# The low halves of V: from VectorE reading PSUM to GpSimd reading a 32-bit copy that ScalarE writes

## The chip, the cores and the metric

The kernel runs on one core of a Trainium2 chip. Its metric is the device time in microseconds (us) of one execution of the whole program, here one launch that holds two attention layers and two feed-forward layers. The engines of the core are called PE (TensorE, matmuls; PEld is its weight load), DVE (VectorE), ACT (ScalarE), POOL (GpSimd) and SP (SyncE, here only an issuer of DMAs).

## The reference

x is 1024 tokens of 256 values. Four blocks follow, each of the form x = x + layernorm(f(layernorm(x))). The change touches the first of them alone:

```
qkv = (x @ w_qkv.T).reshape(B, S, 3 * H, D)          # 16 heads of 128
logits = einsum('bqhd,bkhd->bhqk', q, k) * scale
weights = softmax(logits)
combined = einsum('bhqk,bkhd->bqhd', weights, v).reshape(B, S, H * D)
return combined @ w_out.T
```

The blocks behind it are a feed-forward layer with ternary weights, a causal attention over a latent of 64 values, and a feed-forward layer whose weights are picked from a table of 16 values.

## The kernel before, in words

**Two parts for every operand.** To keep 32-bit accuracy with fast matmuls, each operand is split into a high part, rounded to a short type, and a low part, the remainder. The helper `three` (lines 1096 to 1099) multiplies high by high, high by low and low by high, so every product is three matmuls, whose rows in the profile are L1097, L1098 and L1099. For V the parts are the tiles VH and VL, both 16-bit, 128 partitions by 2 (buffers) by 8 (key blocks) by 256 (two heads). A V projection `("v", h, j)` fills one bank of PSUM with key blocks 2j and 2j+1 of heads h and h+1 (h even), so there are 32 of them. ACT then writes VH from the bank (step `v_hi`, L1505), and DVE reads the bank and VH and writes VL as bank/2048 - VH (step `v_lo`, L1739). The Signal `qkv_lo` says that the low part stands; the bank is free for PE when it does (line 775).

**The first attention, called the heads stage,** takes up the first 590 us or so. It goes through 32 units; a unit is one head with one half of the 1024 queries, and four units make a group of two heads (units 4g to 4g+3). For each unit PE makes four blocks of scores (128 queries by 1024 keys, steps S0 to S3), DVE takes their maxima (M, L1747), ACT the exponentials (e, L1513), DVE the inverse row sums (i, L1755 and L1757), ACT the high part of the weights (h, L1523), DVE their low part (l, L1762), SP transposes both by DMA (L1076), and PE multiplies them by V in eight steps `attend` (A0 to A7, one for each key block). After A7 ACT writes OH (f, L1532) and DVE OL (F, L1821).

**The order** of all this is one list of steps for all engines, written out by hand in `order_of_heads` (lines 169 to 171 hold the letters of a unit). Every engine walks the same list and does, in that order, what is its own; nothing overtakes on an engine. Each unit has five slots (p0 to p4) into which a list of preparation steps is dealt out, one step to a slot. Most of them are steps `lut`, which build the weights of the last layer by picks: DVE (or, for every fourth value, POOL, L2101) compares a tile of indices with one number (L1861), and POOL adds the result to the weight tile (L2106). The tile has 512 columns for the first three tables and 688 for the four later ones. Two pick tiles alternate, so that a pick waits for the add two before it.

**The letters around the change.** X, x and y are a projection, its high part and its low part. In the first unit of a group (4g) X1/x1/y1 are V's key blocks 4 and 5 of this very group, and X2/x2/y2 its blocks 6 and 7; in the second unit (4g+1) they are blocks 0 to 3 of the next group; in the third and fourth units X, x, y are Q and K alone. The end of a unit's list reads

```
p1 w1 y1 w0 h1 S3 M2 p4 A0 A1 X2 A2 A3 l1 p2 e2 x2 i2 A4 M3 A5 A6 h2 y2 l2 w2 p3 e3
```

Step `attend` k waits for the V step j = k // 2 (line 1211): A4 for y1 and A6 for y2 of the same unit, in the first unit of a group; in the later units of the group all of V stands long before. The marks w0, w1 and w2 hold the preparation of weights for later heads. In the first unit of a group w1 is `scale_wv` on POOL (L2073, which waits for VectorE's L1803 of w0) and four squares on ACT (L1471), and w2 is `turn_norm`, `split_wv` (POOL, L2077) and `norm_wqk` (PE L1186, DVE L1781 to L1789, POOL L2046). In the second unit w0 is `split_wqk` (ACT L1478, POOL L2060).

**Banks.** Six of the eight banks hold scores; two serve all else. While a unit's A steps run, one of these two collects the attention's sum, so that every other work product of that time goes through the single bank left.

Of the kernel before, what the change touches and what calls it, by code (L numbers as in the profile page):

```python
# [10 lines left out]
ALU = mybir.AluOpType  # L11
ACT = mybir.ActivationFunctionType
AX = mybir.AxisListType

P = 128
# [12 lines left out]
X_UP = 2.0 ** 11  # L28
# [348 lines left out]
def build(nc, a, out):  # L377
    with ExitStack() as top:
# [16 lines left out]

        with ExitStack() as ctx:
            xh, xl = (sbuf(ctx, n, [P, 2, 1024], F16) for n in ("xh", "xl"))
        XH = sbuf(top, "XH", [P, 2, 1024], F32R)
        XL = sbuf(top, "XL", [P, 2, 1024], F32R)
        ident = sbuf(top, "ident", [P, P])  # L400
# [139 lines left out]
        qkv_hi, exped, e_hi, o_hi = (signal(n, "ACT") for n in ("qkv_hi", "exped", "e_hi", "o_hi"))  # L540
        qkv_lo, maxed, e_lo, o_lo, inverted = (signal(n, "DVE") for n in ("qkv_lo", "maxed", "e_lo", "o_lo", "inverted"))
        o_added, sum_down = signal("o_added", "DVE"), signal("sum_down", "DVE")

        abs_summed, all_summed = signal("abs_summed", "ACT"), signal("all_summed", "PE")
        threshold = signal("threshold", "DVE")
# [124 lines left out]
        for step in HEADS:  # L670
            what, at = step[0], step[1:]
            if mark_norms(*step):
                continue
            if what == "turn_in":
                for k in range(2):
                    for x in (x_turned, x_hi, x_lo):
                        x.mark(at[0], k, at[1])
            elif what in ("split_wqk", "split_wv", "split_wo"):
                kind, h = what.replace("split_w", ""), at[0]
                w_hi.mark(kind, h)  # L680
                w_lo.mark(kind, h)
            elif what == "load_wqk":
                wqk_in[at[0] % 2].mark(*at)
            elif what == "load_wv":
                wv_in.mark(*at)
            elif what == "load_wo":
                wo_in.mark(*at)
            elif what in ("qk", "v"):
                projected.mark(*step)
            elif what in ("qk_hi", "v_hi"):  # L690
                qkv_hi.mark(what[:-3], *at)
            elif what in ("qk_lo", "v_lo"):
                qkv_lo.mark(what[:-3], *at)
            elif what == "scores":
                scored.mark(*at)
            elif what == "max":
                maxed.mark(*at)
            elif what == "exp":
                exped.mark(*at)
            elif what == "row_inv":  # L700
                sum_down.mark(*at)
                inverted.mark(*at)
            elif what == "cast_e":
                e_hi.mark(*at)
            elif what == "rest_e":
                e_lo.mark(*at)
                e_turned[(4 * at[0] + at[1]) % NE_RING].mark(*at)
            elif what == "square_wqk":
                for i in range(4):
                    q_squared.mark(*at, i)  # L710
            elif what == "norm_wqk":
                q_normed.mark(*at)
                q_norm.mark(*at)
                q_power.mark(*at)
                q_factor.mark(*at)
                q_scaled.mark(*at)
                q_scaled.mark(at[0] + 1)
                for i in range(2):
                    q_back.mark(*at, i)
            elif what == "square_wv":  # L720
                v_squared.mark(*at)
            elif what == "scale_wv":
                v_scaled.mark(*at)
            elif what == "norm_wv":
                v_normed.mark(*at)
                v_norm.mark(*at)
                v_power.mark(*at)
                v_factor.mark(*at)
            elif what == "turn_norm":
                norm_turned.mark(*at)  # L730
                v_unit.mark(*at)
            elif what == "attend":
                attended.mark(*at)
            elif what == "finish_hi":
                o_hi.mark(*at)
            elif what == "finish_lo":
                o_lo.mark(*at)
            elif what == "out_proj":
                o_projected.mark(*at)
            elif what == "out_add":  # L740
                o_added.mark(*at)
            elif what == "tern_load":
                raw_in.mark(*at)
            elif what == "abs_sum":
                abs_summed.mark(*at)
            elif what == "threshold":
                all_summed.mark(*at)
                for i in range(4):
                    threshold.mark(*at, i)
            elif what == "ternary":  # L750
                compared.mark(*at)
                tern_set.mark(*at)
            elif what == "lut":
                t, v = at
                if v == 0 and 1 <= t < 6:
                    index_in[(t + 1) % 2].mark(t + 1)
                (picked_g if v % 4 == 3 else picked).mark(t, v)
                if v > 0:
                    SUMS[step] = free_sum[v % 2]
                    free_sum[v % 2] = lut_added.mark(t, v)  # L760
            elif what == "tern_wide":
                (tern_wide_g if at[0] == 0 else tern_wide_v).mark(*at)
            elif what == "up_gate":
                uped.mark(*at, 0)
                uped.mark(*at, 1)
            elif what == "reuse":
                POINT["heads"] = dict(ended)

        for step in HEADS:
            what, at = step[0], step[1:]  # L770
            if what == "turn_in":
                for k in range(2):
                    take_work((*step, k), x_lo[at[0], k, at[1]])
            elif what in ("qk", "v"):
                take_work(step, qkv_lo[step])
            elif what == "scores":
                i = (4 * at[0] + at[1]) % NSB
                BANK[step] = (i, free_scores[i])
                free_scores[i] = e_lo[at]
            elif what == "attend" and at[1] == 0:  # L780
                OB_FREE[at[0]] = free_work[1]
                attending = True
            elif what == "finish_lo":
                free_work[1] = o_lo[at]
                attending = False
                count["work"] += 1
                last_taken[1] = count["work"]
            elif what == "norm_wqk":
                take_work(step, q_norm[at])
            elif what == "norm_wv":  # L790
                take_work(step, v_norm[at])
            elif what == "turn_norm":
                take_work(step, v_unit[at])
            elif what == "out_proj":
                take_work(step, o_added[at])
            elif what == "threshold":
                take_work(step, threshold[at[0], 0])
            elif what == "up_gate":
                BANK[step] = (at[1], [free_scores[at[1]]])
                count["pair"] += 1  # L800
# [292 lines left out]
        def _(e):  # L1093
# [45 lines left out]
            for step in HEADS:  # L1139
# [65 lines left out]
                elif what == "attend":  # L1205
# [2 lines left out]
                    b, vs_ = (h // 2) % 2, slice((h % 2) * P, (h % 2) * P + P)  # L1208
                    for j in range(4):
                        w.wait_ge(*e_turned[(4 * u + j) % NE_RING][u, j])  # L1210
                    w.wait_ge(*qkv_lo["v", h - h % 2, k // 2])
                    if k == 0:
                        w.each([OB_FREE[u]])
                    mm = three(OB, VH[:, b, k, vs_], VL[:, b, k, vs_], ET16[:, u % 2, k, :], ET16[:, u % 2, 8 + k, :],
# [191 lines left out]
        def _(e):  # L1406
# [47 lines left out]
            for step in HEADS:  # L1454
# [44 lines left out]
                elif what == "v_hi":  # L1499
# [3 lines left out]
                    if h >= 4:  # L1503
                        w.wait_ge(*attended[2 * (h - 4) + 3, 7])
                    e.mul(VH[:, (h // 2) % 2, 2 * j:2 * j + 2, :], bank, 1.0 / X_UP).then_inc(qkv_hi.sem, 1)  # L1505
                elif what == "exp":
                    u, j = at
                    c = 4 * (u % 2) + j
# [144 lines left out]
        def _(e):  # L1653
# [59 lines left out]
            for step in HEADS:  # L1713
# [7 lines left out]
                elif what == "qk_lo":  # L1721
# [5 lines left out]
                    if h >= 2:  # L1727
# [1 line left out]
                    e.scalar_tensor_tensor(out=lo[:, h % 2, cs], in0=bank, scalar=UNIT(h, which),  # L1729
                                           in1=f32(hi[:, h % 2, cs]), op0=ALU.mult,  # L1730
                                           op1=ALU.subtract).then_inc(qkv_lo.sem, 1)
                elif what == "v_lo":
                    h, j = at
                    b, js = (h // 2) % 2, slice(2 * j, 2 * j + 2)
                    bank = ps[:, WB + BANK[("v", *at)][0], :].rearrange("p (i n) -> p i n", i=2)
                    w.wait_ge(*qkv_hi[("v", *at)])
                    if h >= 4:
                        w.wait_ge(*attended[2 * (h - 4) + 3, 7])
                    e.scalar_tensor_tensor(out=VL[:, b, js, :], in0=bank, scalar=1.0 / X_UP, in1=VH[:, b, js, :],  # L1739
                                           op0=ALU.mult, op1=ALU.subtract).then_inc(qkv_lo.sem, 1)  # L1740
                elif what == "max":
                    u, j = at
                    c = 4 * (u % 2) + j
# [260 lines left out]
        def _(e):  # L2004
# [30 lines left out]
            for step in HEADS:  # L2035
# [43 lines left out]
                elif what == "split_wo":  # L2079
                    h, = at  # L2080
                    w.wait_ge(*w_hi["o", h])
                    e.tensor_tensor(wol[:, h % NWO, :], wor[:, :], f32(woh[:, h % NWO, :]),
                                    ALU.subtract).then_inc(w_lo.sem, 1)
                elif what == "tern_load":
                    m = at[0]
                    if m > 0:
# [181 lines left out]
```

## Time and profile before

| what | value |
|---|---|
| median of 3 runs | 923.95 us (923.28 to 924.57) |
| span of the profiled execution | 923.3 us |
| PE, PEld busy | 832.7 us, 534.6 us |
| DVE busy | 766.5 us |
| ACT busy | 605.9 us |
| POOL busy | 430.6 us |
| mean granted TensorE clock | 0.987 of full |

The span runs from the first to the last instruction of the profiled execution; it lies within the three runs' times, 0.6 us under their median, so hardly anything lies around it. Busy shares are means over stages with different limits. A busy PE is not a PE at its peak: a 512-column matmul is listed with some 0.38 us, but in a run of them the next starts 0.21 to 0.23 us later.

### The profile page before, as it was taken

The numbers are of one execution on the slowest core, as the hardware profiler recorded it, in microseconds if no ns is written. First come the engines' busy times: TensorE is split into PE (matmuls) and PEld (weight loads), VectorE is DVE, ScalarE is ACT, GpSimd is POOL, SyncE is SP. The second block draws the span as 40 slices with busy tenths as digits, with TensorE's granted clock in tenths as the row PEclk, the third lists the DMA queues.
The fourth block names the chain that finished last, engine by engine and source line by source line (L and its number), as shares of the span: only waits on it lengthen the run. The fifth ranks groups of instructions, "written<-read, shape, count | busy, mean of one in ns | idle before, by whom it ended". The sixth has DMA issues, their size and how long they took to land.

```text
span 923.3 us, 13156 instructions
## 1 busy us (share of the span) xinstructions
PE 832.7 (90%) x4330; PEld 534.6 (58%) x4330; DVE 766.5 (83%) x1597; ACT 605.9 (66%) x1042; POOL 430.6 (47%) x455
## 2 busy tenths in 40 slices
PE   3889999999999999989899998679788999998997
PEld 2555665665665565655565565457555555554686
DVE  3788999889989999999899998585598687876637
ACT  5677767777777676766667767374545767657531
POOL 3134354354445277787667771171323434433301
PEclk9999999999999999999999999799989999999999
DMA  3388858966977667857857668130000000000001
GB/s 122 78 184 156 143 117 190 163 126 136 206 134 153 130 131 144 166 110 144 157 103 132 136 130 159 24 106 0 1 1 1 1 0 2 0 2 1 1 1 45
DMA packets 276867, 86.29 MB, mean 93 GB/s; under 512 B 267584, under 2 KB 272448, under 8 KB 276416
## 3 DMA queue, kind: packets, MB, share of 16 engines
q1 hardware_dynamic: 275520, 80.05, 44.8%
q0 software_dynamic: 992, 5.34, 1.9%
q8 instruction: 34, 0.56, 0.3%
q14 instruction: 33, 0.27, 0.1%
q10 hardware_dynamic: 288, 0.07, 0.0%
HBM read 17.29 MB, written 1.05 MB: 20 GB/s over the span
## 4 chain that ended last, share of the span: by engine, by line
PE 40%; DVE 37%; issue 9%; ACT 8%; DMA 3%; POOL 1%; SPq 1%; POOLq 0%; DVEq 0%; ACTq 0%
DVE EP L1762 9%; DVE nmax L1747 8%; PE ps L1097 7%; PE ps L1099 7%; PE ps L1098 7%; PE ps L1120 4%; DVE ptm L1861 3%; PE ps L1358 3%; PE ps L1344 3%; PE ps L1135 3%; PE ps L1323 3%; DVE ps L1947 2%; DMA ET<-EP 2%; DVE OL L1821 2%; DVE st L1661 1%
## 5 line engine op out<-in xcount | busy, mean ns | idle before, releaser
L1523 ACT ACTIVATE EP<-ps,rinv 128x1024 f16<-128x1024 f32 x128 | 142.2, 1112 | 44.5 <-DVE rinv L1757 42.9
L1762 DVE SCALAR_TENSOR_TENSOR EP<-ps,rinv,EP 128x1024 f16<-128x1024 f32 x128 | 163.3, 1276 | 2.4 <-ACT EP L1523 2.0
L1513 ACT ACTIVATE ps<-ps,nmax 128x1024 f32<-128x1024 f32 x128 | 139.2, 1088 | 35.7 <-DVE nmax L1747 35.2
L1747 DVE TENSOR_REDUCE nmax<-ps 128x1 f32<-128x1024 f32 x128 | 155.0, 1211 | 0.7 <-PE ps L1099 0.7
L1097 PE MATMUL ps<-KH,QH 128*128 128x512 f32 x256 | 115.4, 451 | 8.3 <-DVE KL L1729 4.2
L2106 POOL TENSOR_TENSOR wgu<-wgu,ptm 128x688 f32<-128x688 f32 x60 | 99.7, 1661 | 45.8 <-DVE ptm L1861 43.7
L1097 PE MATMUL ps<-ET,VH 128*128 128x512 f16 x256 | 98.7, 385 | 17.8 <-DMA ET<-EP 14.2
L1099 PE MATMUL ps<-KH,QL 128*128 128x512 f32 x256 | 100.8, 394 | 0.0
L2106 POOL TENSOR_TENSOR wdn<-wdn,ptm 128x512 f32<-128x512 f32 x45 | 57.7, 1282 | 92.2 <-DVE ptm L1861 91.0
L1098 PE MATMUL ps<-KL,QH 128*128 128x512 f32 x256 | 100.5, 392 | 0.0
L1098 PE MATMUL ps<-ET,VH 128*128 128x512 f16 x256 | 98.3, 384 | 0.0
L1099 PE MATMUL ps<-ET,VL 128*128 128x512 f16 x256 | 98.3, 384 | 0.0
L1617 ACT ACTIVATE ET<-ps 128x512 f32<-128x512 f32 (+3 forms) x144 | 62.6, 497 | 37.6 <-PE ps L1344 37.0
L1947 DVE CUSTOM_DVE_ANT_0 ps<-ps,tern 128x512 f32<-128x512 f32 (+3 forms) x128 | 71.9, 603 | 15.5 <-PE ps L1323 15.4
L2013 POOL TENSOR_TENSOR rs<-ve,mhalf 128x4 f32<-128x4 f32 (+2 forms) x22 | 19.8, 898 | 122.4 <-DVE ve L1666 98.2
L1097 PEld LDWEIGHTS ps<-KH,QH 128*128 128x128 f32 x256 | 48.2, 188 | 27.8 <-DVE EP L1762 8.1
L2168 POOL TENSOR_SCALAR_AFFINE_SELECT ET<-ET 128x128 f32<-128x128 f32 x96 | 28.1, 292 | 65.1 <-ACT ET L1617 58.3
L1097 PEld LDWEIGHTS ps<-ET,VH 128*128 128x128 f16 x256 | 25.8, 101 | 54.2 <-DMA ET<-EP 16.2
L1099 PEld LDWEIGHTS ps<-KH,QL 128*128 128x128 f32 x256 | 48.0, 188 | 11.1
L1097 PE MATMUL ps<-xh,wqh 128*128 128x512 f16 x128 | 49.8, 389 | 4.0 <-DVE KL L1729 3.4
L1098 PEld LDWEIGHTS ps<-KL,QH 128*128 128x128 f32 x256 | 48.3, 189 | 7.3
L1098 PE MATMUL ps<-xl,wqh 128*128 128x512 f16 x128 | 49.1, 384 | 0.0
(250 smaller groups left out, 2126.7 us busy)
## 6 DMA issues: line engine op xcount, KB each, us to landing
wqr<-in_wqk SPq DMA_DIRECT2D x16, 256.0 KB, 3.6
wgu<-in_tern POOLq DMA_DIRECT2D x3, 1024.0 KB, 6.1
wvr<-in_wv SPq DMA_DIRECT2D x8, 256.0 KB, 3.9
wor<-in_wo SPq DMA_DIRECT2D x16, 128.0 KB, 3.1
ET<-EP SPq DMA_TRANSPOSE x128, 4.3
X<-in_x SPq DMA_DIRECT2D x2, 512.0 KB, 5.7
prw<-in_down_idx POOLq DMA_DIRECT2D x2, 256.0 KB, 7.0
tern<-in_l_wuq_rep SPq DMA_DIRECT2D x1, 512.0 KB, 4.5
```

Of the source, the lines that this page charges most:

```text
L1097: e.matmul(dst, lh, rh, start=first, stop=False)
L1098: e.matmul(dst, lh, rl, start=False, stop=False)
L1099: return e.matmul(dst, ll, rh, start=False, stop=last)
L1120: mm = e.matmul(ps[:, 2 * r + o, :], l, m, start=i == 0, stop=i == len(pairs) - 1)
L1513: e.activation(bank, bank, ACT.Exp, bias=nmax[:, c:c + 1], scale=1.0, accum_out=rsum[:, c:c + 1]).then_inc(exped.sem, 1)
L1523: e.mul(EP[:, n % NE_RING, 0, :], SB(u, j), rinv[:, c:c + 1]).then_inc(e_hi.sem, 1)
L1617: e.activation(ET[:, r, c:c + n1], ps[:, BANK[(*step, c)][0], n - n1:n], ACT.Exp).then_inc(weight_exped.sem, 1)
L1747: e.tensor_reduce(nmax[:, c:c + 1], SB(u, j), AX.X, ALU.max, negate=True).then_inc(maxed.sem, 1)
L1762: e.scalar_tensor_tensor(out=EP[:, n % NE_RING, 1, :], in0=SB(u, j), scalar=rinv[:, c:c + 1], in1=EP[:, n % NE_RING, 0, :], op0=ALU.mult, ...
L1947: e.tensor_tensor_reduce(src, src, mask[:, m0:m0 + n], 1.0, -3.0e38 if part == 0 else half, ALU.add, ALU.max, NM[:, p % 2, i8, col:col + 1 ...
L2106: e.tensor_tensor(dst, dst, ptm[:, v % 2, 0:n], ALU.add).then_inc(lut_added.sem, 1)
L2168: e.affine_select(out=tile, in_=tile, compare_op=ALU.is_ge, fill=0.0, base=0, pattern=[[1, P]], channel_multiplier=-1).then_inc(masked.sem, 1)
```

## The change

ACT, after it has written VH, reads the same bank again and writes bank/2048 in 32 bits into a new tile VF (two of them, taken in turn by j % 2); POOL then subtracts VH from VF and writes VL. DVE has no part in V any more. VF0 and VF1 lie in memory that the first layer doesn't use at that time. The list of steps is unchanged: ACT's second pass stands in step `v_hi`, and POOL's subtraction at the place of `v_lo`.

- ACT: `v_full`, waits for the POOL step that last read the same VF.
- POOL: `v_lo`, waits for `v_full` (and, from the third group on, for the same attention step as VectorE did).
- PE: a bank of V is free at `v_full` rather than at VectorE's `v_lo`; `attend` waits for POOL's `v_lo`.

```
+            sbuf(ctx, "below_values", [P, 512])
+            VF = [sbuf(ctx, "VF0", [P, 2, 256])]
+            sbuf(ctx, "below_more_values", [P, 512])
+            VF += [sbuf(ctx, "VF1", [P, 2, 256])]
...
+        v_full, v_lo = signal("v_full", "ACT"), signal("v_lo", "POOL")
...
-                take_work(step, qkv_lo[step])
+                take_work(step, qkv_lo[step] if what == "qk" else v_full[at])
...
-                    w.wait_ge(*qkv_lo["v", h - h % 2, k // 2])
+                    w.wait_ge(*v_lo[h - h % 2, k // 2])
...
                     e.mul(VH[:, (h // 2) % 2, 2 * j:2 * j + 2, :], bank, 1.0 / X_UP).then_inc(qkv_hi.sem, 1)
+                    if (h, j) > (0, 1):
+                        w.wait_ge(*v_lo[(h, j - 2) if j > 1 else (h - 2, j + 2)])
+                    e.mul(VF[j % 2][:, :, :], bank, 1.0 / X_UP).then_inc(v_full.sem, 1)
...
-                elif what == "v_lo":
-                    h, j = at
-                    b, js = (h // 2) % 2, slice(2 * j, 2 * j + 2)
-                    bank = ps[:, WB + BANK[("v", *at)][0], :].rearrange("p (i n) -> p i n", i=2)
-                    w.wait_ge(*qkv_hi[("v", *at)])
-                    if h >= 4:
-                        w.wait_ge(*attended[2 * (h - 4) + 3, 7])
-                    e.scalar_tensor_tensor(out=VL[:, b, js, :], in0=bank, scalar=1.0 / X_UP, in1=VH[:, b, js, :],
-                                           op0=ALU.mult, op1=ALU.subtract).then_inc(qkv_lo.sem, 1)
...
+                elif what == "v_lo":
+                    h, j = at
+                    b, js = (h // 2) % 2, slice(2 * j, 2 * j + 2)
+                    w.wait_ge(*v_full[at])
+                    if h >= 4:
+                        w.wait_ge(*attended[2 * (h - 4) + 3, 7])
+                    e.tensor_tensor(VL[:, b, js, :], VF[j % 2][:, :, :], VH[:, b, js, :],
+                                    ALU.subtract).then_inc(v_lo.sem, 1)
```

## Rows read from the trace of the kernel before

**Rows 1.** The page: part 1, busy us (share) xinstructions; part 2, DVE in 40 slices.

```profile
PE 832.7 (90%) x4330; PEld 534.6 (58%) x4330; DVE 766.5 (83%) x1597; ACT 605.9 (66%) x1042; POOL 430.6 (47%) x455
...
DVE  3788999889989999999899998585598687876637
```

**Rows 2.** Busy time by stretch, one group of units: from:to, us, each engine, clock, DMA.

```profile
396.00:470.00 74.00, 68.19 (x344) 42.35 (x344) 68.85 (x107) 50.07 (x78) 55.08 (x37) 0.98 0.71 134
```

**Rows 3.** Groups of instructions by line and shape: busy us, mean ns, idle before.

```profile
L1739 DVE SCALAR_TENSOR_TENSOR VL<-ps,VH 128x512 f16<-128x512 f32 x32 | 21.9, 686 | 3.9 <-ACT VH L1505 3.9
L1505 ACT ACTIVATE VH<-ps 128x512 f16<-128x512 f32 x32 | 18.9, 595 | 21.5 <-PE ps L1099 21.5
```

**Rows 4.** One line's instructions: duration ns min/median/max (L1446, L2060, L1861).

```profile
L1446 ACT ACTIVATE XN<-ps,tsc x4: 687/688/690, 626.6 to 658.5; 128x512 f32<-128x512 f32 x4
...
L2060 POOL TENSOR_TENSOR wql<-wqr,wqh x16: 1149/1158/1519, 16.8 to 506.1; 128x512 f16<-128x512 f32 x16
...
L1861 DVE TENSOR_SCALAR ptm<-prw,lut x44: 468/558/1882, 68.7 to 549.1; 128x512 f32<-128x512 int32 x22, 128x688 f32<-128x688 int32 x22
```

**Rows 5.** Timeline of POOL in unit 20: start us, us, instruction, [idle before <-releaser].

```profile
397.16 1.26 POOL L2073 TENSOR_TENSOR wvr<-wvr,vs 128x512 f32<-128x512 f32 x1 [0.56 <-DVE vs L1803]
398.41 2.58 POOL L2101 TENSOR_SCALAR ptm<-prw,lut 128x688 f32<-128x688 int32 x1
401.07 3.42 POOL L2106 TENSOR_TENSOR wgu<-wgu,ptm 128x688 f32<-128x688 f32 x2
```

**Rows 6.** Timeline of unit 20: A6 on PE, then DVE and ACT up to OL.

```profile
401.92 0.39 PE L1097 MATMUL ps<-ET,VH 128*128 128x512 f16 x1 [0.55 <-DVE VL L1739]
...
403.64 0.16 DVE L1781 TENSOR_SCALAR wnorm<-ps 128x4 f32<-128x4 f32 x1 [0.48 <-PE ps L1186]
403.83 0.69 DVE L1784 TENSOR_SCALAR wpow<-wnorm 128x4 int32<-128x4 int32 x1
404.56 1.09 DVE L1789 TENSOR_SCALAR wfac<-wpow 128x4 int32<-128x4 int32 x1
...
404.31 0.69 ACT L1532 ACTIVATE OH<-ps,vinv 128x512 fp32r<-128x512 f32 x1 [1.40 <-PE ps L1099]
...
406.31 0.75 DVE L1821 SCALAR_TENSOR_TENSOR OL<-ps,vinv,OH 128x512 fp32r<-128x512 f32 x1
```

**Rows 7.** Timeline of POOL in units 4, 12, 16, 28: its last work before y2's place.

```profile
122.92 1.27 POOL L2106 TENSOR_TENSOR wdn<-wdn,ptm 128x512 f32<-128x512 f32 x1
...
261.28 1.27 POOL L2106 TENSOR_TENSOR wdn<-wdn,ptm 128x512 f32<-128x512 f32 x1 [1.82 <-DVE ptm L1861]
...
333.60 0.59 POOL L2095 DMA_DIRECT2D prw<-in_gate_idx  x1 [0.30 <-POOL wdn L2106]
...
542.16 3.43 POOL L2106 TENSOR_TENSOR wgu<-wgu,ptm 128x688 f32<-128x688 f32 x2
```

**Rows 8.** Timeline of PE in units 4, 12, 16: A6; of DVE in unit 28: y2.

```profile
125.30 0.39 PE L1097 MATMUL ps<-ET,VH 128*128 128x512 f16 x1 [1.11 <-DVE VL L1739]
...
263.35 0.39 PE L1097 MATMUL ps<-ET,VH 128*128 128x512 f16 x1 [0.39 <-DVE VL L1739]
...
333.36 0.39 PE L1097 MATMUL ps<-ET,VH 128*128 128x512 f16 x1 [0.21 <-DVE VL L1739]
...
542.40 0.68 DVE L1739 SCALAR_TENSOR_TENSOR VL<-ps,VH 128x512 f16<-128x512 f32 x1
```

**Rows 9.** Timeline of ACT and DVE in unit 17, a group's second unit.

```profile
345.27 1.12 ACT L1523 ACTIVATE EP<-ps,rinv 128x1024 f16<-128x1024 f32 x1
...
347.12 1.28 DVE L1762 SCALAR_TENSOR_TENSOR EP<-ps,rinv,EP 128x1024 f16<-128x1024 f32 x1
348.32 1.88 DVE L1861 TENSOR_SCALAR ptm<-wgu,lut 128x688 f32<-128x688 int32 x1
```

**Rows 10.** A PE wait in the timeline, then the stretch behind it (columns as in rows 2).

```profile
451.61 0.59 PE L1097 MATMUL ps<-ET,VH 128*128 128x512 f16 x1 [2.44 <-DMA ET<-EP]
...
451.40:454.80 3.40, 3.19 (x8) 1.19 (x9) 2.60 (x5) 0.30 (x2) 3.26 (x2) 0.50 0.70 150
```

More of the change, by code:

```diff
@@ L689, in build @@
                 projected.mark(*step)
[L690 to L693, printed above, removed]
+            elif what == "qk_hi":
+                qkv_hi.mark("qk", *at)
+            elif what == "v_hi":
+                qkv_hi.mark("v", *at)
+                v_full.mark(*at)
+            elif what == "qk_lo":
+                qkv_lo.mark("qk", *at)
+            elif what == "v_lo":
+                v_lo.mark(*at)
             elif what == "scores":
@@ L2083, in _ @@
                                     ALU.subtract).then_inc(w_lo.sem, 1)
+                elif what == "v_lo":
+                    h, j = at
[5 more added lines that the diff above has]
+                                    ALU.subtract).then_inc(v_lo.sem, 1)
                 elif what == "tern_load":
```

## The prediction

> **What bounds the kernel now.** I read the busy times first, then the slices, then one group of units by stretch, and last the timelines around each V step. In the heads stage VectorE is close to full: nines in nearly every slice up to the 22nd [rows 1], and 68.85 of the 74 us of units 20 to 23, while ScalarE has 50.07 and GpSimd 55.08 [rows 2]. PE's 68.19 us there is inflated by the listed lengths of pipelined matmuls, but it too has little air. So VectorE's time is worth having, if what replaces it isn't waited for. Whether it is, is a question of places: GpSimd has time on average, but in the first unit of each group its work is dense just where y2 stands [rows 5].
>
> **What goes.** VectorE loses 32 steps `v_lo` of 0.686 us: 21.9 us, and 3.9 us of idle time that it spent before them on ScalarE's VH [rows 3]. That is the ceiling of the gain, 25.8 us. What else changes about 0.2% (1.8 us) or more is counted below; less than that a measurement of this kernel can't tell from no change.
>
> **What ScalarE gets.** 32 passes from PSUM to 32 bits, 128x512. Not in the trace as such; the nearest are VH itself (595 ns, 16-bit output [rows 3]) and a 32-bit copy out of PSUM (688 ns [rows 4]). I take 0.69: 22 us in all. ScalarE idled 21.5 us before its VH steps alone [rows 3], so on the average it has room, but the pass is at a bad place: it stands behind VH and ahead of h1 (ScalarE's high part of the weights), for which VectorE's l1 waits. In unit 17 h1 began at 345.27, took 1.12, and l1 began at 347.12 [rows 9]. Moved back by 0.69, h1 ends at 347.08, and l1 can't start sooner than before, though y1 is gone ahead of it. So the first of a unit's two removed steps is worth nothing. The second (y2) has only maxima ahead of the next l, and h2 there waits for VectorE: it is worth its slot, about 0.6, and the idle time goes too. I take 0.7 for each of the seven units 4g+1 that have V steps: 5 us gained. Ends: 0 and 1.6 each. In units 4g+2 and 4g+3 nothing changes. The bank of V comes free at ScalarE's second pass, 0.69 behind VH, about when VectorE would have been through: nothing. The prologue's two steps trade 1.4 us of VectorE for 1.4 of ScalarE, which l3 waits for: nothing.
>
> **What GpSimd gets.** 32 subtractions, 16-bit out of a 32-bit and a 16-bit tile, 128x512. GpSimd does just this form already, for the weights: 1.149 / 1.158 / 1.519 us [rows 4]. I take 1.16 and 0.08 between two instructions, 1.24 each, 40 us in all on an engine that is 47% busy [rows 1]. Sixteen of them (both steps of units 4g+1 and the prologue's) are for a later group and nobody waits. The others are y1 and y2 of units 4g, needed by A4 and A6 of the same unit.
>
> *y1*: GpSimd's scale step in unit 20 ends at 398.42 [rows 5]; y1 would end at 399.7. A6's own wait began at 401.92 - 0.55 = 401.37 [rows 6], and A4 stands six matmuls of some 0.21 us ahead of that, at about 400.1. In time, barely.
>
> *y2*: this is where it fails. Ahead of y2 on GpSimd stand, in unit 20, y1, the pick of p4 (2.58 us) and two adds (3.42 us), which end at 404.49 now [rows 5]. With y1 and y2 put in, y2 ends 2.4 later, at 406.9. A6 runs at 401.92 now, already held up by VectorE's y2 [rows 6]: it comes **5.0 us late**. The same sum, last work of GpSimd plus 2.4 against A6 now [rows 7, 8]: unit 4, 124.19 + 2.4 - 125.30 = 1.3 (unit 8 is of this kind: 1.3 again); unit 12, where GpSimd idles 1.82 us and so swallows y1, 262.55 + 1.25 - 263.35 = 0.5; unit 16, with the issue of an index DMA, 334.19 + 2.4 - 333.36 = 3.2; unit 24 repeats unit 20, 5.0; unit 28, 545.59 + 2.4 against y2's end of 543.08 and A6 some 0.3 later, 4.6. Unit 0 has no table work: 0.2. Sum: 21.1 us.
>
> Does it reach the end? Behind A6 on PE stand the two small matmuls of w2, A7 and the next unit's scores. VectorE has l2 left and then waits for w2's matmul, as it does for 0.48 us today [rows 6], and soon for OH, which ScalarE begins 2.4 us behind A6. So both full engines stand still, and nothing queued can be done meanwhile. Two things give some back. VectorE's small steps of w2 took 0.69 and 1.09 us in unit 20, where an instruction of that size takes 0.16 [rows 6], because they collided with GpSimd's work. Later they don't: 1.4 us less in units 20 and 24, so OL slips by 3.6 rather than 5.0. And GpSimd's chain starts at the scale step, which waits for VectorE [rows 5] and comes earlier without y1 on VectorE: between 0 and 0.6, I take 0.3 in six units. 21.1 - 2.8 - 1.8 = 16.5 us.
>
> **The ports.** The longest pick of VectorE, 1.88 us at 348.32 where the median is 0.56, began while an add of GpSimd ran [rows 4, 9]: the two engines shut each other out. VectorE's old `v_lo`, with one operand in PSUM, never idled for GpSimd [rows 3]. I put no term for it into the sum, since removing VectorE work also spaces things out; the worst is a rival below. The Trainium skill, page "SBUF — State Buffer", section "Who interferes with whom", says that a VectorE operation in a two-port mode and a GpSimd operation hold a shared port pair in turn, each for its whole instruction, and that a VectorE instruction with at most one SBUF input doesn't contend. By that rule the change puts 32 more locks where none were, and the sum would be some 5 us higher.
>
> **The clock.** PE waited 2.44 us before 451.61, and the granted clock was 0.50 for the 3.4 us from 451.40 on [rows 10]: 1.2 GHz instead of 2.4, half of 3.4 us of matmul time lost, 1.7 us. The new waits before A6 in units 16, 20, 24 and 28 are longer than that one. Lower end 0 (none falls, or the loss is hidden), upper end 6.8 (all four); I take two, 3.4 us.
>
> **The sum.** 923.3 (the profiled execution) + 16.5 - 5 + 3.4 = 938.2. That execution lay 0.6 under the median, so I say 939.
>
> **The rivals.**
>
> *A. GpSimd is in time (faster).* If y2 were ready at A6 in most units, VectorE's removed time would count. The place is y2 on GpSimd, the price its wait. It decides where GpSimd's last work before y2 ends over 1.2 us before VectorE's y2 would. Unit 0 is near to that, unit 12 not quite, the other six not. For it: GpSimd is only 47% busy. Against it: rows 5 and 7. With no wait and 0.7 + 0.7 gained in each of 15 units it gives 923.9 - 21 = 903; with half the waits, 915. Chance 0.12.
>
> *B. A wash.* The waits of the early units cost under 1 us and later ones are partly regained by PE or VectorE catching up in units 4g+1 to 4g+3, 11 us regained beyond my 5, and no clock loss: 922 to 926. Against it: VectorE has but 5 of 74 us idle in such a group [rows 2]. Chance 0.05.
>
> *C. Worse: ports and clock.* The new GpSimd instructions shut out picks. If a quarter of 32 does so for up to 1.3 us (1.88 - 0.56), that is 10 us on the full engine, and all four clock losses add 3.4 more: 939 + 10 + 3.4 = 952. For it: such picks are frequent in units with the 688-wide tables. Against it: a pick can only be in the way once, and waits before A6 hide some. The page cited above states this lock as a rule. Chance 0.15.
>
> *Forecast.* The wait before A6, as summed: 931 to 948, by its ends (the gain in units 4g+1 up to 11, clock 0 to 6.8, the chain's start 0 to 0.6). Chance 0.68.
>
> So slower by over 0.2%: 0.68 + 0.15 = 0.83; within 0.2%: 0.05; faster: 0.12. The range leaves out A and the top of C: 922 to 951.
>
> **What the profile of the changed kernel would show.** VectorE busy 22 us less, ScalarE 22 more (0.69 each), GpSimd 37 more (1.16 each). Before A6 in units 4g, PE idle with GpSimd's VL as releaser, under 1 us in units 0 and 12, 3 in 16, some 5 in 20, 24 and 28, 20 us or so in all. VectorE with new idle time before L1812 and L1781 behind it. In units 4g+1 l1 waits for h1. The clock at half for a few us after the long waits. Half a dozen us less between units 4g+1 and 4g+2. I am wrong if A6 starts right behind A5 in units 20, 24 and 28 (then GpSimd was quicker or its order other than I read), or if it waits and the next OL is not later (then there was slack that I don't see).

## The result, and the profile after it

The changed kernel took 954.56 us in the median of four runs (949.85 to 958.13), the one before 924.26 beside it: a ratio of 1.031, 95% interval 1.029 to 1.034. Slower, as forecast, but by 30 us where 15 were forecast, and above the stated range. Run again it gave 1.0315 (1.028 to 1.035). The profiled execution, with a span of 948.1 us, is the fastest of its four, so the two traces differ by 24.8 us (948.1 against 923.3) and not by 30.

The page of the changed kernel, as [rows 1], with the clock and the parts that answer to [rows 3]:

```profile
span 948.1 us, 13203 instructions
...
PE 841.8 (89%) x4330; PEld 539.7 (57%) x4330; DVE 753.0 (79%) x1565; ACT 620.5 (65%) x1074; POOL 471.1 (50%) x487
...
PEclk9999989999999999989989989799989999999999
...
L1766 DVE SCALAR_TENSOR_TENSOR EP<-ps,rinv,EP 128x1024 f16<-128x1024 f32 x128 | 163.4, 1277 | 13.5 <-ACT EP L1536 12.4
...
L1107 PE MATMUL ps<-ET,VH 128*128 128x512 f16 x256 | 99.9, 390 | 37.8 <-POOL VL L2094 26.5
...
L1545 ACT ACTIVATE OH<-ps,vinv 128x512 fp32r<-128x512 f32 x32 | 22.0, 688 | 45.8 <-PE ps L1109 45.8
```

Three things stand in it. VectorE is busy 13.5 us less (753.0 against 766.5), though 32 instructions of 0.686 us, 21.9 us, are gone. PE waits 26.5 us for GpSimd's VL. And the clock's row has four eights in the heads stage that weren't there.

The new instructions by line in the changed kernel (ns min/median/max): ScalarE's pass was 0.1 us shorter than I took it (0.59 for 0.69), GpSimd's subtraction just what the weights' split had promised [rows 4]. The last two lines are those who waited for GpSimd's subtraction (us, times):

```profile
L1518 ACT ACTIVATE VF<-ps x32: 591/593/617, 41.1 to 559.5; 128x512 f32<-128x512 f32 x32
...
L2094 POOL TENSOR_TENSOR VL<-VF,VH x32: 1148/1160/1602, 42.8 to 565.2; 128x512 f16<-128x512 f32 x32
...
  PEld ps L1107: 30.3, 8
  PE ps L1107: 26.5, 7
```

Unit 20 again, as [rows 5] and [rows 6]: the timeline of GpSimd, then PE, VectorE and two stretches by engine of the changed kernel.

```profile
407.81 1.27 POOL L2077 TENSOR_TENSOR wvr<-wvr,vs 128x512 f32<-128x512 f32 x1 [0.56 <-DVE vs L1807]
409.04 1.16 POOL L2094 TENSOR_TENSOR VL<-VF,VH 128x512 f16<-128x512 f32 x1
410.18 2.96 POOL L2113 TENSOR_SCALAR ptm<-prw,lut 128x688 f32<-128x688 int32 x1
413.22 3.41 POOL L2118 TENSOR_TENSOR wgu<-wgu,ptm 128x688 f32<-128x688 f32 x2
416.59 1.15 POOL L2094 TENSOR_TENSOR VL<-VF,VH 128x512 f16<-128x512 f32 x1
```

```profile
411.56 0.38 PE L1109 MATMUL ps<-ET,VL 128*128 128x512 f16 x1
417.80 0.61 PE L1107 MATMUL ps<-ET,VH 128*128 128x512 f16 x1 [5.86 <-POOL VL L2094]
418.20 0.63 PE L1108 MATMUL ps<-ET,VH 128*128 128x512 f16 x1
...
419.72 0.16 DVE L1816 TENSOR_SCALAR vinv<-ps 128x2 f32<-128x2 f32 x1 [6.23 <-PE ps L1213]
420.56 0.16 DVE L1785 TENSOR_SCALAR wnorm<-ps 128x4 f32<-128x4 f32 x1 [0.68 <-PE ps L1196]
420.76 0.17 DVE L1788 TENSOR_SCALAR wpow<-wnorm 128x4 int32<-128x4 int32 x1
...
422.58 0.75 DVE L1825 SCALAR_TENSOR_TENSOR OL<-ps,vinv,OH 128x512 fp32r<-128x512 f32 x1 [0.71 <-ACT OH L1545]
```

```profile
408.00:411.60 3.60, 3.60 (x25) 2.13 (x22) 3.44 (x6) 3.60 (x6) 3.60 (x3) 1.00 0.04 9
...
417.00:423.80 6.80, 5.75 (x16) 3.44 (x16) 2.12 (x8) 1.69 (x2) 4.36 (x5) 0.50 0.03 7
```

The order on GpSimd is the one foretold: scale step, y1, pick, two adds, y2. A6 waits 5.86 us for y2, and VectorE stands idle for 6.23 us behind it. What I had half left out is the last line: when PE goes on, its clock stands at one half, 1.2 GHz, for 6.8 us. The matmuls of A6 start 0.40 us apart instead of 0.21, and OL begins 4.8 us behind A6; it was 4.4 before [rows 6], of which 1.4 were the two hindered small steps that run freely now (0.17).

Such falls of the clock come after other waits too, and their length doesn't go by that of the wait. In unit 4 of the same trace PE had waited half as long:

```profile
127.20 0.61 PE L1107 MATMUL ps<-ET,VH 128*128 128x512 f16 x1 [2.91 <-POOL VL L2094]
...
127.00:133.80 6.80, 6.35 (x17) 3.59 (x18) 3.35 (x9) 1.84 (x3) 4.33 (x6) 0.51 0.53 100
```

GpSimd too stood still, 23.4 us in seven steps, for ScalarE's VF (POOL VL L2094 <- ACT VF L1518 among this kernel's waits). Hardly anyone waited for what this put off: VectorE stood 1.1 us in all before its picks for GpSimd's adds.

### The profile page after: what moved, and what is told of

It reads as the page before. It is cut to its first block, busy times and chain, and to the rows that moved or that the text cites. A ratio compares the mean times of both kernels' runs of the same rounds, so it can differ in the third digit from the quotient of the medians.

```text
span 948.1 us, 13203 instructions
## 1 busy us (share of the span) xinstructions
PE 841.8 (89%) x4330; PEld 539.7 (57%) x4330; DVE 753.0 (79%) x1565; ACT 620.5 (65%) x1074; POOL 471.1 (50%) x487
## 4 chain that ended last, share of the span: by engine, by line
PE 38%; DVE 27%; issue 13%; POOL 10%; ACT 9%; DMA 2%; SPq 0%; POOLq 0%; DVEq 0%; ACTq 0%
PE ps L1107 7%; PE ps L1108 6%; PE ps L1109 6%; DVE EP L1766 6%; DVE nmax L1751 4%; PE ps L1130 4%; PE ps L1368 3%; DVE ps L1951 3%; DVE ptm L1865 3%; PE ps L1145 3%; PE ps L1354 3%; POOL wgu L2118 3%; PE ps L1333 2%; POOL ptm L2113 2%; POOL VL L2094 2%
## 5 line engine op out<-in xcount | busy, mean ns | idle before, releaser
L1766 DVE SCALAR_TENSOR_TENSOR EP<-ps,rinv,EP 128x1024 f16<-128x1024 f32 x128 | 163.4, 1277 | 13.5 <-ACT EP L1536 12.4
L1107 PE MATMUL ps<-ET,VH 128*128 128x512 f16 x256 | 99.9, 390 | 37.8 <-POOL VL L2094 26.5
L1107 PE MATMUL ps<-KH,QH 128*128 128x512 f32 x256 | 118.6, 463 | 7.6 <-DVE KL L1742 3.9
L1108 PE MATMUL ps<-ET,VH 128*128 128x512 f16 x256 | 100.1, 391 | 0.0
L1545 ACT ACTIVATE OH<-ps,vinv 128x512 fp32r<-128x512 f32 x32 | 22.0, 688 | 45.8 <-PE ps L1109 45.8
```

The source lines that it names most:

```text
L1107: e.matmul(dst, lh, rh, start=first, stop=False)
L1108: e.matmul(dst, lh, rl, start=False, stop=False)
L1766: e.scalar_tensor_tensor(out=EP[:, n % NE_RING, 1, :], in0=SB(u, j), scalar=rinv[:, c:c + 1], in1=EP[:, n % NE_RING, 0, :], op0=ALU.mult, ...
```

## The experiments

There are eleven runs: ten further kernels, and the changed one once more. Where a ratio stands below, the kernel before, run beside it, is 1, and 0.001 is 0.92 us. Medians of runs that weren't taken side by side are compared by their ratios.

### The relief of VectorE alone

```
-                    w.wait_ge(*qkv_lo["v", h - h % 2, k // 2])
+                    w.wait_ge(*qkv_hi["v", h - h % 2, k // 2])
...
-                    mm = three(OB, VH[:, b, k, vs_], VL[:, b, k, vs_], ET16
+                    mm = three(OB, VH[:, b, k, vs_], VH[:, b, k, vs_], ET16
...
-                elif what == "v_lo":
...
```

> This kernel leaves the low part of V out: nobody writes VL, PE multiplies VH in its place (the same matmuls), V's bank is free at VH. It has the change's relief of VectorE and none of its burdens. If VectorE's time is what bounds the heads stage in both kinds of units, it gains most of the 22 to 26 us: 898 to 905. If the relief is worth only one of two steps in the units 4g+1 (my working: the other is waited for by ScalarE), 908 to 915. If VectorE's relief is worth nothing because PE or ScalarE paces, 920 to 924.

Measured: 920.17 us, ratio 0.994 (0.992 to 0.996): 5.3 us gained, close to the case in which the relief is worth nothing. So the whole prize of the change was 5 us, not 22. Where the rest went shows in VectorE's busy time, first of this kernel, then the line of the small step `vp<-vs` of w0 in it, then that of VectorE's low part of the weights (l) with its waits; the last two lines are `vp<-vs` and VectorE's waits at l in the kernel before:

```profile
PE 831.6 (91%) x4330; PEld 535.2 (58%) x4330; DVE 755.0 (82%) x1565; ACT 605.2 (66%) x1042; POOL 431.4 (47%) x455
...
L1791 DVE TENSOR_SCALAR vp<-vs 128x256 int32<-128x256 int32 x8 | 7.2, 905 | 0.3
...
L1753 DVE SCALAR_TENSOR_TENSOR EP<-ps,rinv,EP 128x1024 f16<-128x1024 f32 x128 | 163.3, 1277 | 9.3 <-ACT EP L1523 8.2
...
L1800 DVE TENSOR_SCALAR vp<-vs x8: 293/297/847, 26.5 to 469.7; 128x256 int32<-128x256 int32 x8
...
DVE EP L1762 <- ACT EP L1523: 2.0, 7, 0.4
```

VectorE lost 32 instructions, but only 11.5 us of busy time (766.5 to 755.0). Others got longer, by 10.4 us in all. `vp<-vs` took 3.7 us in its eight instructions before (median 0.297) and takes 7.2 now, 0.905 in the mean: in unit 20, with y1 gone, it starts 0.3 us behind the start of GpSimd's add of p1 instead of 1.0, and so meets more of it. The picks of the 688-wide tables take 2.4 us more, the step behind `wnorm` 1.4. The other drain is ScalarE: VectorE's l waited 8.2 us for h instead of 2.0. On ScalarE h stands behind V's high part, which waits for PE's projection. So the first of a unit's two removed steps was worth little even without a second pass of ScalarE, to which my working had put that down.

### ScalarE's pass alone

```
                     e.mul(VH[:, (h // 2) % 2, 2 * j:2 * j + 2, :], bank, 1.0 / X_UP).then_inc(qkv_hi.sem, 1)
+                    e.mul(VF[j % 2][:, :, :], xh[:, :, 0:256], 1.0).then_inc(v_full.sem, 1)
```

> The kernel before, with 32 extra ScalarE passes (128x512, 32-bit output, read from SBUF) behind VH and nothing else moved; VectorE still makes VL. My working puts ScalarE's pass on the path of h1 in front of a VectorE that has no air: 0.6 us at the first V step of each of 15 units, 8 to 10 us, 932 to 934. Rival: ScalarE's idle time takes it, 923 to 926.

Measured: 929.90, ratio 1.0046 (1.0023 to 1.007): 4.3 us, half of what I expected and more than the rival allowed. The pass isn't free. (These passes read 16-bit x from SBUF and took 0.62 us each, 0.03 more than the change's passes out of PSUM, and V's bank isn't held by them.) Then the same passes behind the next h:

> The kernel before with the 32 extra ScalarE passes again, now behind h instead of ahead of it. If it is the place and not ScalarE's load that cost 4.3 us, the kernel is within 1 us of the one before, 924 to 926.5. If the load costs, it stays at 929 to 930.

Measured: 927.73, ratio 1.0020 (1.0007 to 1.0033), 1.8 us. Less, and the intervals of the two just overlap; the place seems to account for half, but that isn't settled.

### GpSimd's load alone

```
+                elif what == "v_lo":
+                    h, j = at
+                    b, js = (h // 2) % 2, slice(2 * j, 2 * j + 2)
+                    w.wait_ge(*vf_set[0])
+                    w.wait_ge(*x_hi[0, 1, 1])
+                    e.tensor_tensor(VL[:, b, js, :], VF0[:, :, :], xh[:, :, 0:256], ALU.subtract).then_inc(v_lo.sem, 1)
```

> The kernel without a low part of V (920.2) plus 32 GpSimd subtractions of the change's size at the change's places, which read tiles that always stand and for which nobody waits. So it has the relief of VectorE and GpSimd's load, but no wait of PE and no second pass of ScalarE. If the two engines shut each other out as the split kernels say (3.9 us for 14 subtractions), 6 to 10 us over 920.2, 926 to 930. If the loads don't meet, 920 to 922.

Measured: 932.52, ratio 1.0072 (1.0051 to 1.0093), against 0.9943 without the subtractions: 0.0129, 12 us, more than either theory said. Nobody waits for these results. What they cost comes either from VectorE instructions that take longer beside them, or from GpSimd's own later steps, which they put off. By line in this kernel, and last a wait of its own:

```profile
PE 830.7 (89%) x4330; PEld 534.7 (58%) x4330; DVE 762.1 (82%) x1565; ACT 605.9 (65%) x1042; POOL 471.9 (51%) x488
...
L1857 DVE TENSOR_SCALAR ptm<-wgu,lut 128x688 f32<-128x688 int32 x22 | 21.7, 988 | 1.3 <-POOL wgu L2109 1.3
L1857 DVE TENSOR_SCALAR ptm<-prw,lut 128x688 f32<-128x688 int32 x22 | 20.4, 928 | 2.5 <-POOL wgu L2109 2.5
L1839 DVE SCALAR_TENSOR_TENSOR tern<-wgu,tsc,tern 128x512 bf16<-128x512 f32 x12 | 13.7, 1140 | 0.4
...
DVE wgu L1853 <- POOL wgu L2109: 2.0, 1, 2.0
```

VectorE's busy time rose by 7.1 us with the same 1565 instructions (755.0 to 762.1). And it waited 5.8 us for adds that came late, 3.8 before its picks into the two pick tiles and 2.0 once before the first pick of a table; the kernel without the subtractions has no such wait. So by these two sums over half of the 12 us is lengthening and the rest queueing. Unlike the change's subtractions, these don't wait for ScalarE, and may stand a little earlier.

### GpSimd's V ahead of its table steps

```
...
+        if step[0] == "v_lo" and step[2] == 2:
+            holding = True
+        elif step[0] == "v_lo" and step[2] == 3:
+            todo += late
...
```

While `holding` is set, between y1 and y2 of a group's first unit, steps `lut` go into `late`; they follow y2.

> The changed kernel with one thing moved: in the first unit of each group GpSimd does y2 ahead of the table steps of p4 and p2, which follow it. If the loss is GpSimd's queue ahead of y2, PE's waits before A6 (some 26 us in all) fall under 1 us each, the clock doesn't fall there, and the time drops to 905 to 925, less a wait of VectorE's p3 pick for the late add (up to 1.5 us in three units). If the loss is the subtraction's length or ScalarE's pass, the time stays above 940.

Measured: 939.70, ratio 1.016 (1.012 to 1.020), 14.9 us. Half of the loss went with the order alone, and half stayed, where I had expected 905 to 925. The waits before A6 did nearly what I expected (1.3 us at most, where I had said under 1): in this kernel PE's waits for VL are 4.1 us in all instead of 26.5 (they were 3.2 for VectorE's VL before the change), and the clock doesn't fall in the heads stage. In their place VectorE waits for the adds put off:

```profile
DVE ptm L1880 <- POOL wgu L2133: 10.9, 6, 3.4
...
PE ps L1122 <- POOL VL L2109: 4.1, 6, 1.3
```

With a third pick tile as well (`ptm[:, v % 3, 0:n]`, and the sums freed by v % 3):

> GpSimd's y2 ahead of the table steps as in the run before, and a third pick tile, so that a pick of VectorE no longer waits for the add two before it (10.9 us of VectorE idle there, 6 times). If these waits are what was left of the loss, 939.7 drops by 8 to 11 us, to 929 to 932; what remains over the kernel before is ScalarE's pass (4.3 us alone) and shut-out picks. If they are not on the path, it stays at 938 to 942.

Measured: 934.42, ratio 1.0106 (1.008 to 1.013): 5.1 us less by the ratios, half of the expected. One wait of VectorE for an add is left among this kernel's waits, at the first pick of the last table:

```profile
DVE wgu L1876 <- POOL wgu L2133: 3.8, 1, 3.8
```

What stays, 9.8 us over the kernel before, has hardly any wait before A6 in it (PE waits 4.0 us for VL, against 3.2 before), but may have that one in it. It is near the three single parts: -5.3 + 4.3 + 12 = 11.

### The clock alone

```
+FILL = {4: 12, 8: 10, 12: 6, 16: 14, 20: 26, 24: 26, 28: 21}
...
+                    if k == 6 and u in FILL:
+                        w.wait_ge(*zero_set[0])
+                        for _ in range(FILL[u]):
+                            e.matmul(OB, zero[:, 0:P], ET16[:, u % 2, 0, :], start=False, stop=False)
                     w.wait_ge(*v_lo[h - h % 2, k // 2])
```

> The changed kernel with 115 extra matmuls (zero weights, added to the attention's sum, so they change nothing) that fill most of PE's wait before A6 in the units 4, 8, 12, 16, 20, 24 and 28. GpSimd's y2 ends when it did, so the waiting itself is the same. If the falls of the clock behind these waits cost what my ledger leaves to them, the clock stays at full there and the time drops by 5 to 12 us against the changed kernel, to 942 to 949. If the clock costs nothing, it stays within 2 us of the changed kernel, or is longer by what the extra matmuls overrun.

> The changed kernel itself once more, on the same chip as the next three: 950 to 958, PE waits before A6 of the units 4g of 24 to 27 us, and a granted clock of one half for 27 to 35 us within the heads stage.

Measured: the changed kernel 953.56, with the filled waits 941.81 (ratio 1.020, 1.018 to 1.023). By the medians 11.8 us, by the ratios 10.4 went by giving PE 115 useless matmuls. The page of the filled kernel:

```profile
span 939.7 us, 13434 instructions
...
PE 855.8 (91%) x4445; PEld 545.5 (58%) x4445; DVE 754.7 (80%) x1565; ACT 620.1 (66%) x1074; POOL 471.3 (50%) x488
...
PEclk9999999999999999999999999799989999999999
```

The delay of A6 against A4, over that of the kernel before, is 23.2 us in seven units here and 23.5 in the changed kernel: the waits are the same, the falls are gone. So the price of the falls is 10.4 to 11.8 us, over a third of the whole loss. The changed kernel's own runs point the same way: over its first four, span and mean clock go together (948.1 us at 0.972, 952.3 and 953.4 at 0.970, 956.4 at 0.968). How many of the seven waits bring a fall, and for 3.4 or 6.8 us, differs between the two traces of the changed kernel: behind the waits of units 20, 24 and 28 (4.8 to 5.9 us) it was 6.8 us each time, behind the other four (1.4 to 3.4 us) none, 3.4 or 6.8. In all the clock stood at half for 30.7 us of the heads stage in the first trace and 37.5 in the repeat, where I had expected 27 to 35.

### V on GpSimd only where nobody waits

```
+def on_pool(h, j):
+    return h > 0 and j < 2
```

> VL of the steps that nobody waits for (second units of a group, 14 steps) goes over ScalarE and GpSimd as in the changed kernel; the first units' and the prologue's stay on VectorE as before. If my term for the second units is right (0.7 each, seven units), 917 to 920. If the relief is eaten by ScalarE's pass and by shut-out picks, 923 to 926. No PE wait on GpSimd's VL in either case.

Measured: 925.14, ratio 0.999 (0.997 to 1.001): no difference. Neither the 5 us that I had booked for the second units, nor a loss. Two follow-ups, first without GpSimd's 14 subtractions (the low part of V is left out there, and the attention takes VH a second time for those blocks), then with ScalarE's pass behind h:

> The split kernel without its 14 GpSimd subtractions (ScalarE's pass stays): it leaves out the low part of V in the blocks made in the second units; PE multiplies VH in its place. VectorE's relief and ScalarE's burden are those of the split kernel, which came out even with the one before. If GpSimd's instruction shuts out VectorE's picks and so eats the relief, this is 3 to 6 us faster than the split kernel, 919 to 922. If ScalarE's pass or PE eats it, the same as the split kernel, 924 to 926.

> The split kernel (second units' VL over ScalarE and GpSimd, the rest on VectorE) with ScalarE's second pass put behind the next high part of the weights (h1, h2) instead of ahead of it. If the pass ahead of h1 is what takes the relief in the second units, 1 to 3 us under the split kernel, 922 to 924. If GpSimd's locks take it alone (removing the subtraction gave 3.9 us), the same as the split kernel, 925.

Measured: without the subtractions 921.23, ratio 0.996 (0.994 to 0.999); with the pass behind h 927.11, ratio 1.001 (1.000 to 1.002), no gain, where 1 to 3 us had been one of the two cases. So some relief seems to be there, 3 us, and GpSimd's subtraction to take it back. The difference to the split kernel, 0.0028, lies just inside the joint width of the two intervals (0.0031), so the times alone don't show it; it has the sign of the run with GpSimd alone, and VectorE's busy time is 4.6 us longer with the 14 subtractions than without (765.4 against 760.8). No gain from another place of ScalarE's pass shows here. No version that computes the whole of V beats the kernel before: what was left to gain is under the cost of moving it.

## Why the prediction was half right

**The mechanism was right.** GpSimd's queue in the first unit of each group makes A6 late, and PE and VectorE stand still together. The lateness came out as summed, 23.5 us in seven units for 21.1 in eight: 1.0 in unit 12 (forecast 0.5), 1.8 and 2.0 in units 4 and 8 (1.3), 3.2 in 16 (3.2), 5.3, 5.2 and 5.0 in 20, 24 and 28 (5.0, 5.0, 4.6). The small steps behind it gave back 2.9 us of their length, 2.8 forecast. The rival with GpSimd in time falls, as does the wash. The size was wrong, 30 us instead of 15, and two steps of the sum failed.

**The first step that failed: the clock was mis-sized.** It was "I take two, 3.4 us", two falls of 3.4 us, each costing half. The filled kernel says 10.4 to 11.8. There were five new falls in the profiled run (seven in the repeat), most of them 6.8 us long, as in the 417.00 stretch above. I had sized all from the one fall behind a 2.4 us wait [rows 10], and had looked for falls only in units 16, 20, 24 and 28; in one trace or the other they came behind the waits of units 4, 8 and 12 too (2.9, 2.4 and 1.4 us). I had called four falls of that size the upper end.

**The second: everything beside waits and clock stood at a gain of 5 us, and it was a loss.** The sum had "- 5" for VectorE's relief in the second units, nothing for ScalarE's passes in the first ones, and nothing for what GpSimd's new instructions do to its neighbours ("I put no term for it into the sum, since removing VectorE work also spaces things out"). Three kernels that ran side by side split the loss by their ratios:

| from | to | us |
|---|---|---|
| the kernel before, 1 | V ahead of the table steps, three pick tiles, 1.0106 | +9.8 |
| that | the changed kernel with filled waits, 1.0202 | +8.9 |
| that | the changed kernel, 1.0315 | +10.4 |

The first row is the change nearly without its waits and falls: +9.8 us instead of -5. The single runs name what is in it: the relief is 5.3 us as a whole, the subtractions alone cost 12, ScalarE's passes alone 4.3. In the second units the 5 us booked as gained weren't: the split kernel shows 0.7, with an interval around none. I had counted ScalarE there, but not GpSimd's own instruction, which runs in those units too. The second row is what the late A6 adds at full clock, 7.4 us by the medians and 8.9 by the ratios, with some 3 us of noise either way, for the 16.5 forecast.

**The two costs hide each other.** The 12 us of the subtractions alone can't simply be added to the waits. VectorE's busy time is 755.0 us without the subtractions, 762.1 with them alone, 762.1 again with the queue removed, but only 754.7 with the filled waits and 753.0 in the changed kernel. So where VectorE stands still behind A6, GpSimd's instructions lengthen its own hardly at all; where it doesn't, they do. If these 7.4 us (762.1 less 754.7) counted in full, the waits by themselves would be worth 8.9 + 7.4 = 16.3 us, close to the 16.5 of the forecast. That is an estimate, since busy time is not time on the path, and no run shows it. How waits, lengthened instructions and ScalarE's passes share the first units stays open.

One such meeting in the changed kernel; its GpSimd timeline, then VectorE's:

```profile
405.59 1.67 POOL L2118 TENSOR_TENSOR wgu<-wgu,ptm 128x688 f32<-128x688 f32 x1 [2.86 <-DVE ptm L1865]
```

```profile
405.88 1.53 DVE L1804 TENSOR_SCALAR vp<-vs 128x256 int32<-128x256 int32 x1
```

An instruction that takes 0.29 us at its shortest begins in GpSimd's add, and ends 0.15 behind the add's end. The Trainium skill's page "SBUF — State Buffer", section "Who interferes with whom", states this as an exclusive lock held for a whole instruction. The trace agrees: 1.53 is what is left of the add (1.38) plus the rest. My own sentence on that section was too wide: it exempts VectorE instructions with at most one SBUF input only outside the two-port modes. The picks and `vp<-vs`, which read one tile from SBUF, are the very ones that were held up here (1.88 us and 1.53). Nor does a hindered instruction show as idle time, as I read [rows 3]; it shows in its length. The old `v_lo` was never hindered by that measure either (0.679 to 0.693 us). The 5 us that I put beside the sum by this rule had no working shown.

**Luck.** Of the rivals C, ports and clock together at 952, came nearest to 954.6; I had given it 0.15. That is luck in part: it had the clock at 6.8 us in all, under the measured 10.4 to 11.8, and added 10 us of hindered picks on top of the full waits, which the busy times above speak against.

**Small slips that decided nothing.** The ends of the terms, taken together, span 928 to 949 and not 931 to 948. Of VectorE's first 22 slices 14 are nines, six are eights. And the span of 923.3 lies within the three times by accident: in each run recorded with both, the time is 1.7 to 1.9 us longer than the span.

## What to carry to other kernels

Before work goes from a full engine to a half-empty one, look at the receiver's queue at the place of the step, not at its share of busy time: here 16 of 32 steps had slack, but eight of the rest, the y2, had up to 6 us of table work ahead of them. Price what the receiver's new instructions do to their neighbours: here 32 GpSimd subtractions that nobody waited for cost 12 us, 7.1 of them in longer VectorE instructions. And when a change makes PE wait for some microseconds, add what the clock takes afterwards (10.4 to 11.8 us here, for seven waits); filler matmuls into the wait are a quick way to measure that.

## What I had not expected of the hardware

Filling a wait with matmuls of zero weights kept the granted clock at full through seven waits, and took 11.8 us off (953.56 to 941.81). The length of the wait did not tell that of the fall: after a PE wait of 5.86 us and after one of 2.91 us the clock was at half for 6.8 us, after one of 2.44 for 3.4 [rows 10]. And a removed VectorE instruction was not worth its length: 32 of 0.686 us took 11.5 us off VectorE's busy time and 5.3 us off the whole. In the case looked at, `vp<-vs` in unit 20, the cause is that the instruction moved into one of GpSimd's; for the other lengthened ones that is likely, but not shown.
